# A macaron transformer layer on one core: queries' and keys' transfers behind a block's first loads, and a gap between the last scatter of a segment and its block

## The chip, the cores and the metric

One core of a Trainium2 chip runs the whole program. The metric is the device time of one execution in microseconds (us), as the median of several runs.

## The reference

Tokens are 32 batches of 256 rows with 128 features, so 8192 tokens or 64 tiles of 128. The layer has three parts, each with a residual:

```
x = x + 0.5 * moe(layernorm(x))        # 12 experts, 2 per token; 8 are real, 4 pass the token through
x = x + attention(layernorm(x))        # 16 heads of 8, scores + lambda * prior(|i - j|), softmax
x = x + 0.5 * moe(layernorm(x))        # the same weights again
```

A real expert is `silu(x @ w1.T) @ w2.T` with 256 hidden units. A token's two experts are the two largest gate logits, and their weights are a softmax over those two.

## The kernel before

**Segments and blocks.** The tokens of the first moe are cut into segments 0 to 4 (8, 8, 16, 16, 16 tiles) and those of the second into segments 5 to 9 (16, 16, 16, 8, 8). For each segment the kernel routes the tokens, scatters their normed rows into a table `xg` in DRAM that is sorted by expert (two indirect DMAs for each tile, `scatter_rows`, issued by GpSimd), and works through the table in groups of 256 rows (`experts`): 15 groups for a segment of 8 tiles, 23 for one of 16. Then it gathers each token's two result rows from a table `yg` (`gather_rows`, again two indirect DMAs for each tile) and adds them with their weights (`combine`, on VectorE). The passage through one segment's groups is called a block here, by the segment's number.

**A group in a block.** SyncE (SP) loads 256 rows transposed (`load_cols`, L313, into one of RX = 6 buffers `x_cols`). TensorE does `up` (L446 to L448), ScalarE does `silu` twice (L743, L745), VectorE subtracts to get the low part (L1168), TensorE does `down` two groups later (L461 to L464), ScalarE takes the result out of PSUM (`take_y`, L751, into one of RY = 4 buffers `y_rows`), and SP stores it (`store_y`, L322). SP issues in the written order: load g, then store g - 9. So store 0 comes behind load 9, and `take_y` of group 4 needs the buffer of store 0. Load g waits until `up` of group g - 6 is done.

**The next segment is routed inside a block.** VectorE takes the moments at its group 4, GpSimd computes the reciprocal root (`token_root`, L853 and L856), VectorE norms four tiles with each of its groups from 6 on (`token_norm`, L1052 and on), TensorE transposes them from its group 8 on (L396) and computes gate logits.

**Attention turns.** Attention runs in turns b = -1 to 32, one for each batch, each with 8 steps. A step has two score tiles of batch b (L548), two raw score tiles for the row maxima (L540), the prior added by matmuls (L573), exponentials (L807), maxima (L1276) and the product with the values (L602). The semaphore `st_done` counts 16 score tiles for each turn, and GpSimd's scatters and gathers are paced by it (`spread`). Each turn also projects the queries and keys of batch b + 2. SP then stores them (`keep_rows`) and reads them back in another layout with six DMAs (`operand_rows`, L353), into `k_op` and `q_in`. They are first read at step 3 of turn b + 1. `operand_rows(b + 2)` waits until all scores of turn b are done.

**Blocks among turns.** Turns and blocks share all engines, and each engine runs its program in the written order. `PHASES` says ahead of which turn a block stands and which segment it routes. Before a block, SP issues the block's first six loads at the end of its work for the turn, then `operand_rows`:

```
for b in range(-1, NBATCH - 2):
    if b in PHASES:
        experts(PHASES[b][0], RX)
    keep_rows(b + 2)
    if b + 1 in PHASES:
        for g in range(RX):
            load_cols(PHASES[b + 1][0], g)
    operand_rows(b + 2)
```

The first of these loads waits for all scatters of the segment (`scattered`). GpSimd's order is a list by hand. `spread(rows, q, t0, t1, b, steps, first)` issues the DMAs of tiles t0 to t1 evenly over `steps` steps from step `first` of turn b, with the norm of a coming batch (`batch_norm`, four instructions) once in each turn. `beside_block` issues them inside a block, and `norm_turns` only does the norms. `ADDS` says in which turns VectorE combines which tiles.

Of the kernel before, what the change touches and what calls it, by code (L numbers as in the profile page):

```python
# [43 lines left out]
def build(nc, x, wq, bq, wk, bk, wv, bv, wo, bo, lam, gate, ebias, w1, w2, ident, tri, prior, out, reach):  # L44
# [24 lines left out]
    RX, RY = 6, 4  # L69
# [5 lines left out]
    def through(counts):  # L75

        total = [0]
        for c in counts:
# [4 lines left out]
    T0 = through(n for _, n in SEG)  # L83
    K0 = through(n // 4 for _, n in SEG)

    PHASES = {4: (2, 3), 7: (3, 4), 11: (4, 5), 17: (5, 6), 25: (6, 7), 29: (7, 8)}

    ADDS = {-1: (0, 4, 8), 0: (1, 0, 2), 1: (1, 2, 6), 2: (1, 6, 8), 4: (2, 0, 4), 7: (2, 8, 12), 8: (2, 12, 16),
            29: (6, 0, 8), 30: (6, 8, 16)}
    for first, q in ((11, 3), (17, 4), (23, 5)):  # L90
        for i in range(4):
            ADDS[first + i] = (q, 4 * i, 4 * i + 4)

# [13 lines left out]
    with ExitStack() as ctx:  # L107
# [164 lines left out]
        def _(sp):  # L272
# [35 lines left out]
            def load_cols(q, g):  # L308
                n = G0[q] + g
                if g == 0:  # L310
                    sp.wait_ge(scattered[q % 2], landed(q))
                wait(sp, C["up_done"], n + 1 - RX)
                sp.dma_start_transpose(x_cols[:, n % RX], xg[q][g * GS:(g + 1) * GS, :]).then_inc(cols_in[n % RX], 16)  # L313
# [15 lines left out]
            out_tiles = out.rearrange("(n p) d -> p n d", p=P)  # L329
            AHEAD = RX + 3  # L330

            def experts(q, begun=0):
                for g in range(groups[q] + AHEAD):
                    if begun <= g < groups[q]:
                        load_cols(q, g)
                    if g >= AHEAD:
                        store_y(q, g - AHEAD)

# [8 lines left out]
            def operand_rows(b):  # L347

                sp.wait_ge(kq_out, 32 * (b + 1))
                wait(sp, A["st_done"], 16 * (b - 1))  # L350
                for dst, which, parts in ((k_op, 1, (0, 0, 1)), (q_in, 0, (0, 1, 0))):
                    for r in range(3):
                        sp.dma_start(  # L353
                            dst[r::4, b % 2, :, :],
                            kq_kept[:, 2 * parts[r] + which, :].rearrange("(g i) c -> i g c", g=G)).then_inc(kq_in[b % 2], 16)
# [8 lines left out]
            operand_rows(0)  # L364
            for b in range(-1, NBATCH - 2):
                if b in PHASES:
                    experts(PHASES[b][0], RX)
                keep_rows(b + 2)
                if b + 1 in PHASES:
                    for g in range(RX):  # L370
                        load_cols(PHASES[b + 1][0], g)
                operand_rows(b + 2)
                if b == 27:
                    store_out(5)
            store_out(6)
            experts(8)
# [458 lines left out]
        def _(pool):  # L835
# [130 lines left out]
            def norm_turns(b0, b1):  # L966
                for b in range(b0, b1):
                    batch_norm(b + 3)
# [6 lines left out]
            attention_constants()  # L975
            beside_block(gather_rows, 0, 0, 8, 1)
            norm_turns(-3, 0)
            spread(gather_rows, 1, 0, 8, 0, 16)
            spread(scatter_rows, 2, 0, 16, 2, 16)
            token_root(3)  # L980
            spread(gather_rows, 2, 0, 4, 4, 4)
            spread(scatter_rows, 3, 0, 16, 4, 20, 4)
            beside_block(gather_rows, 2, 4, 16, 3)
            spread(scatter_rows, 4, 0, 16, 7, 32)
            beside_block(gather_rows, 3, 0, 12, 4)
            spread(gather_rows, 3, 12, 16, 11, 8)
            spread(scatter_rows, 5, 0, 16, 12, 32)
            norm_turns(16, 17)
            beside_block(gather_rows, 4, 0, 12, 5)
            spread(gather_rows, 4, 12, 16, 17, 8)  # L990
            spread(scatter_rows, 6, 0, 16, 18, 32)
            spread(gather_rows, 5, 0, 12, 22, 24)
            beside_block(gather_rows, 5, 12, 16, 6)
            spread(scatter_rows, 7, 0, 16, 25, 32)
            beside_block(gather_rows, 6, 0, 16, 7)
            spread(scatter_rows, 8, 0, 8, 29, 8)
            spread(gather_rows, 7, 0, 12, 30, 16)
# [438 lines left out]
```

## Time and profile before

| | |
|---|---|
| median of 3 runs | 1392.34 us |
| lowest, highest | 1388.91, 1397.88 us |
| profiled execution | 1403.38 us, its span 1401.3 us |
| granted TensorE clock, mean | 0.88 |
| PE busy | 1003.8 us (72%) |
| DVE busy | 933.3 us (67%) |
| ACT busy | 665.9 us (48%) |
| POOL busy | 620.3 us (44%) |
| DMA | 125.29 MB, mean 89 GB/s |

PE is TensorE (PEld its weight loads), DVE VectorE, ACT ScalarE, POOL GpSimd, SP SyncE. Busy times leave out register, semaphore and DMA-issuing instructions; SPq and POOLq are the queues of those engines. Starts are counted from the beginning of the span, and L12 is line 12 of the kernel before.

### The profile page before, as it was taken

To read this page: it belongs to the slowest core of one execution; us is meant where nothing else is said; L and a number is where in the kernel's file an instruction comes from. 1 tells how busy PE (TensorE), PEld (TensorE's weight loads), DVE (VectorE), ACT (ScalarE), POOL (GpSimd) and SP (SyncE) were. 2 spreads that over 40 slices of the span, in tenths; PEclk is the share of its full clock that TensorE was granted. 3 is DMA by queue.
4 is the path that set the end of the run, shared out by engine and by line. 5 is a ranking of instruction groups with operands and counts; after the bars stand their busy time and mean duration, and the time that the engine had idled before them with its cause. 6 is when DMAs were issued, how large, how long until landed. Compare 5 with 4: busy or idle time off the path is not lost.

```text
span 1401.3 us, 37446 instructions
## 1 busy us (share of the span) xinstructions
PE 1003.8 (72%) x13558; PEld 658.8 (47%) x13558; DVE 933.3 (67%) x2505; ACT 665.9 (48%) x1356; POOL 620.3 (44%) x685
## 2 busy tenths in 40 slices
PE   1468177768776788688888888888888787775650
PEld 1346134447444744474445644444754464333540
DVE  5637476557665778578887778878688745646432
ACT  0146034346444655565555655555664554442540
POOL 2745135530555445444542555454224445541346
PEclk9979569889897989889999999999799978875985
DMA  8235812134113611262113721123431264140563
GB/s 246 70 103 126 256 41 60 54 80 107 54 52 90 139 47 58 75 143 69 47 58 72 148 73 47 58 58 81 106 84 49 84 140 101 50 86 18 117 155 74
DMA packets 248880, 125.29 MB, mean 89 GB/s; under 512 B 124384, under 2 KB 238925, under 8 KB 248448
## 3 DMA queue, kind: packets, MB, share of 16 engines
q1 hardware_dynamic: 232320, 94.01, 26.3%
q0 software_dynamic: 16384, 28.89, 8.6%
q8 instruction: 116, 1.90, 0.6%
q14 instruction: 60, 0.49, 0.1%
HBM read 36.25 MB, written 65.31 MB: 72 GB/s over the span
## 4 chain that ended last, share of the span: by engine, by line
PE 39%; DVE 25%; issue 14%; ACT 5%; POOL 5%; DMA 4%; another core or an unknown queue 4%; SPq 4%; POOLq 0%; DVEq 0%; ACTq 0%
DVE row_max L1276 9%; PE banks L573 8%; PE banks L602 4%; PE banks L548 3%; PE banks L446 3%; PE banks L448 2%; PE banks L405 2%; POOL big L888 2%; PE banks L540 2%; PE banks L447 2%; DVE h_lo L1168 2%; DMA x_cols<-xg 2%; PE banks L461 2%; PE banks L464 2%
## 5 line engine op out<-in xcount | busy, mean ns | idle before, releaser
L807 ACT ACTIVATE probs<-banks 128x512 f32<-128x512 f32 x512 | 279.5, 595 | 329.8 <-PE banks L573 301.8
L888 POOL DMA_INDIRECT big<-yg,slots x256 | 255.4, 998 | 384.2 <-ACT y_rows L751 184.9
L1276 DVE TENSOR_REDUCE row_max<-banks 128x2 f32<-128x512 f32 x512 | 330.4, 685 | 99.3 <-PE banks L573 73.2
L874 POOL DMA_INDIRECT xg<-xs,slots x256 | 259.5, 1014 | 277.5 <-PE banks L573 180.6
L1168 DVE TENSOR_TENSOR h_lo<-h_f,h_hi 128x512 bf16<-128x512 f32 x198 | 135.6, 688 | 182.1 <-ACT h_hi L745 154.5
L602 PE MATMUL banks<-probs,v_op 128*32 128x256 f32 x2048 | 196.9, 405 | 6.5 <-ACT probs L807 2.0
L461 PE MATMUL banks<-w_all,h_hi 128*128 x792 | 161.4, 231 | 52.5 <-DVE h_lo L1168 21.1
L540 PE MATMUL banks<-k_op,q_in 32*128 32x256 bf16 x1024 | 154.2, 290 | 57.8 <-DVE row_max L1276 39.9
L548 PE MATMUL banks<-q_op,k_op 32*128 32x256 bf16 x1024 | 151.3, 288 | 59.5 <-issue 45.2
L573 PE MATMUL banks<-band_parts,thirds 96*32 96x296 bf16 (+2 forms) x4096 | 184.0, 288 | 0.4 <-issue 0.4
L743 ACT ACTIVATE h_f<-banks 128x512 f32<-128x512 f32 x198 | 119.4, 603 | 130.4 <-PE banks L448 94.9
L446 PE MATMUL banks<-x_cols,w_all 128*128 128x256 bf16 x396 | 119.7, 302 | 78.0 <-DMA x_cols<-xg 47.1
L463 PE MATMUL banks<-w_all,h_hi 128*128 x792 | 157.0, 231 | 0.2
L464 PE MATMUL banks<-w_all,h_lo 128*128 x792 | 156.1, 230 | 1.3 <-issue 1.2
L573 PEld LDWEIGHTS banks<-band_parts,thirds 96*32 96x32 bf16 x4096 | 100.1, 98 | 62.1 <-issue 61.9
L751 ACT ACTIVATE y_rows<-banks 128x256 f32<-128x256 f32 x198 | 77.7, 393 | 102.6 <-PE banks L464 54.6
L448 PE MATMUL banks<-x_cols,w_all 128*128 128x256 bf16 x396 | 119.9, 303 | 0.9 <-issue 0.9
L447 PE MATMUL banks<-x_cols,w_all 128*128 128x256 bf16 x396 | 120.1, 303 | 0.4 <-issue 0.4
L745 ACT ACTIVATE h_hi<-banks 128x512 bf16<-128x512 f32 x198 | 119.4, 603 | 0.0
L461 PEld LDWEIGHTS banks<-w_all,h_hi 128*128 128x128 bf16 x792 | 82.3, 104 | 75.4 <-issue 71.3
L548 PEld LDWEIGHTS banks<-q_op,k_op 32*128 32x128 bf16 x1024 | 51.4, 92 | 130.9 <-issue 107.8
L602 PEld LDWEIGHTS banks<-probs,v_op 128*32 128x32 f32 x2048 | 81.7, 115 | 20.3 <-issue 13.3
(170 smaller groups left out, 1632.2 us busy)
## 6 DMA issues: line engine op xcount, KB each, us to landing
yg<-y_rows SPq DMA_DIRECT2D x198, 128.0 KB
k_op<-kq_kept SPq DMA_DIRECT2D x96, 64.0 KB
q_in<-kq_kept SPq DMA_DIRECT2D x96, 64.0 KB
xg<-zeros SPq DMA_DIRECT2D x2, 2944.0 KB, 14.4
xg<-xs,slots POOLq DMA_INDIRECT x256
big<-yg,slots POOLq DMA_INDIRECT x256
kq_kept<-kq_hi SPq DMA_DIRECT2D x32, 128.0 KB
kq_kept<-kq_lo SPq DMA_DIRECT2D x32, 128.0 KB
```

The source lines that it names most:

```text
L446: pe.matmul(o, w_hi, hi, start=True, stop=False)
L461: pe.matmul(o, h_hi[:, n % 4, cols], w_hi, start=c == 0 and j == 0, stop=False, skip_group_check=True)
L464: mm = pe.matmul(o, h_lo[:, n % 4, cols], w_hi, start=False, stop=c == 1, skip_group_check=True)
L540: return pe.matmul(banks[:, MX[v % 2], bass.ts(k, L)], q_in[r:r + 32, par, g, bass.ts(qt, P)], k_op[r:r + 32, par, g, :], start=k == 0, st ...
L548: return pe.matmul(banks[:, ST[(16 * b + u) % 3], bass.ts(k, L)], k_op[r:r + 32, par, g, bass.ts(kt, P)], q_op[r:r + 32, g, :], start=k == ...
L573: return pe.matmul(banks[32 * r:32 * r + 32, bank, :].rearrange("p (k c) -> p k c", k=2)[:, :, c0:c1], thirds[:], bc(band_parts[:, first:f ...
L602: mm = pe.matmul(banks[32 * j:32 * j + 32, PV, bass.ts(k, L)], v_op[:, par, kt, J * (2 * gp + k) + j, :], probs[:, w // 2 % 2, j, bass.ts( ...
L807: act.activation(probs[:, q % 2, u % 4, :], banks[:, ST[(16 * b + u) % 3], :], ACT.Exp).then_inc(A["exp_done"], 1)
L874: pool.indirect_dma_start(xg[q], bass.IndirectOffsetOnAxis(slots[:, q % 4, c, t:t + 1], 0), xs[:, q % 2, t, :], None, bounds_check=groups[ ...
L888: pool.indirect_dma_start(y_back[:, i, c, :], None, yg[q], bass.IndirectOffsetOnAxis(slots[:, q % 4, c, t:t + 1], 0)).then_inc(gathered[i] ...
L1168: dve.tensor_tensor(h_lo[:, n % 4, :], h_f[:, n % 3, :], h_hi[:, n % 4, :], ALU.subtract).then_inc(C["lo_ready"], 1)
L1276: dve.tensor_reduce(row_max[:, gp, :, qt, j], banks[:, MX[v % 2], :].rearrange("p (k c) -> p k c", k=2), AX.X, ALU.max).then_inc(A["max_do ...
```

## The change

The blocks that stood ahead of turns 11 and 17 stand ahead of turns 12 and 18. `ADDS` and the GpSimd list follow. In the GpSimd list the last scatter of a segment now comes before the end of the turn ahead of its block: for segments 2 and 3 in step 4 of that turn, for segment 4 a whole turn earlier (5 had this already), for segment 7 in step 3. For this, the scatters of segments 2 and 3 and the gathers of segment 1 are closer together in turns 0 to 6. Ahead of a block, SP no longer issues `operand_rows` behind the first six loads. It issues them inside the block, behind load 12 and ahead of store 3. The store of the finished segment 5 moves one turn back, behind the first loads of block 7.

```diff
-    PHASES = {4: (2, 3), 7: (3, 4), 11: (4, 5), 17: (5, 6), 25: (6, 7), 29: (7, 8)}
+    PHASES = {4: (2, 3), 7: (3, 4), 12: (4, 5), 18: (5, 6), 25: (6, 7), 29: (7, 8)}
...
-    for first, q in ((11, 3), (17, 4), (23, 5)):
+    for first, q in ((12, 3), (18, 4), (24, 5)):
...
-            def experts(q, begun=0):
+            def experts(q, begun=0, b=None):
                 for g in range(groups[q] + AHEAD):
                     if begun <= g < groups[q]:
                         load_cols(q, g)
+                    if b is not None and g == AHEAD + 3:
+                        operand_rows(b)
                     if g >= AHEAD:
                         store_y(q, g - AHEAD)
...
                 if b in PHASES:
-                    experts(PHASES[b][0], RX)
+                    experts(PHASES[b][0], RX, b + 1)
                 keep_rows(b + 2)
                 if b + 1 in PHASES:
                     for g in range(RX):
                         load_cols(PHASES[b + 1][0], g)
-                operand_rows(b + 2)
-                if b == 27:
+                else:
+                    operand_rows(b + 2)
+                if b == 28:
                     store_out(5)
...
-            spread(gather_rows, 1, 0, 8, 0, 16)
-            spread(scatter_rows, 2, 0, 16, 2, 16)
+            spread(gather_rows, 1, 0, 8, 0, 11)
+            spread(scatter_rows, 2, 0, 16, 1, 18, 3)
+            norm_turns(3, 4)
             token_root(3)
             spread(gather_rows, 2, 0, 4, 4, 4)
-            spread(scatter_rows, 3, 0, 16, 4, 20, 4)
+            spread(scatter_rows, 3, 0, 16, 4, 17, 4)
+            norm_turns(6, 7)
             beside_block(gather_rows, 2, 4, 16, 3)
             spread(scatter_rows, 4, 0, 16, 7, 32)
+            norm_turns(11, 12)
             beside_block(gather_rows, 3, 0, 12, 4)
-            spread(gather_rows, 3, 12, 16, 11, 8)
-            spread(scatter_rows, 5, 0, 16, 12, 32)
-            norm_turns(16, 17)
+            spread(gather_rows, 3, 12, 16, 12, 8)
+            spread(scatter_rows, 5, 0, 16, 13, 32)
+            norm_turns(17, 18)
             beside_block(gather_rows, 4, 0, 12, 5)
-            spread(gather_rows, 4, 12, 16, 17, 8)
-            spread(scatter_rows, 6, 0, 16, 18, 32)
-            spread(gather_rows, 5, 0, 12, 22, 24)
-            beside_block(gather_rows, 5, 12, 16, 6)
-            spread(scatter_rows, 7, 0, 16, 25, 32)
+            spread(gather_rows, 4, 12, 16, 18, 8)
+            spread(scatter_rows, 6, 0, 16, 19, 32)
+            spread(gather_rows, 5, 0, 8, 23, 16)
+            beside_block(gather_rows, 5, 8, 16, 6)
+            spread(scatter_rows, 7, 0, 16, 25, 28)
+            norm_turns(28, 29)
```

## Rows read from the trace of the kernel before

**Rows 1.** Timeline of PE, first matmul of blocks 2 to 7 (start, us, idle before)

```profile
293.59 0.39 PE L446 MATMUL banks<-x_cols,w_all 128*128 128x256 bf16 x1 [8.26 <-DMA x_cols<-xg]
...
433.90 0.39 PE L446 MATMUL banks<-x_cols,w_all 128*128 128x256 bf16 x1 [7.37 <-DMA x_cols<-xg]
...
579.40 0.39 PE L446 MATMUL banks<-x_cols,w_all 128*128 128x256 bf16 x1 [5.41 <-DMA x_cols<-xg]
...
761.33 0.28 PE L446 MATMUL banks<-x_cols,w_all 128*128 128x256 bf16 x1 [1.82 <-issue]
...
979.11 0.39 PE L446 MATMUL banks<-x_cols,w_all 128*128 128x256 bf16 x1 [2.37 <-issue]
...
1120.04 0.39 PE L446 MATMUL banks<-x_cols,w_all 128*128 128x256 bf16 x1 [5.29 <-DMA x_cols<-xg]
```

**Rows 2.** Timeline of SP at block 2

```profile
290.93 7.78 SPq L313 DMA_TRANSPOSE x_cols<-xg  x6
298.82 2.65 SPq L353 DMA_DIRECT2D k_op<-kq_kept  x3
...
303.45 5.19 SPq L313 DMA_TRANSPOSE x_cols<-xg  x4
308.69 0.58 SPq L322 DMA_DIRECT2D yg<-y_rows  x1
```

**Rows 3.** Timeline of SP at block 6

```profile
981.52 5.20 SPq L313 DMA_TRANSPOSE x_cols<-xg  x4
986.81 1.07 SPq L322 DMA_DIRECT2D yg<-y_rows  x1
```

**Rows 4.** Timeline of PE, group 6 of blocks 2, 4 and 7

```profile
306.28 0.39 PE L446 MATMUL banks<-x_cols,w_all 128*128 128x256 bf16 x1 [3.07 <-DMA x_cols<-xg]
...
592.82 0.39 PE L446 MATMUL banks<-x_cols,w_all 128*128 128x256 bf16 x1 [3.88 <-DMA x_cols<-xg]
...
1132.77 0.39 PE L446 MATMUL banks<-x_cols,w_all 128*128 128x256 bf16 x1 [2.71 <-issue]
```

**Rows 5.** Timeline of ACT: group 4 in blocks 2 and 6, 7 in 6

```profile
310.83 0.38 ACT L751 ACTIVATE y_rows<-banks 128x256 f32<-128x256 f32 x1 [1.97 <-DMA yg<-y_rows]
...
989.51 0.38 ACT L751 ACTIVATE y_rows<-banks 128x256 f32<-128x256 f32 x1
...
997.82 0.38 ACT L751 ACTIVATE y_rows<-banks 128x256 f32<-128x256 f32 x1 [1.00 <-PE banks L464]
```

**Rows 6.** Line L751, blocks 2, 5, 6, 7: ns of one, first to last start

```profile
L751 ACT ACTIVATE y_rows<-banks x23: 384/385/416, 299.2 to 351.0; 128x256 f32<-128x256 f32 x23
...
L751 ACT ACTIVATE y_rows<-banks x23: 384/390/431, 765.4 to 813.2; 128x256 f32<-128x256 f32 x23
...
L751 ACT ACTIVATE y_rows<-banks x23: 384/384/415, 983.8 to 1034.2; 128x256 f32<-128x256 f32 x23
...
L751 ACT ACTIVATE y_rows<-banks x23: 377/385/465, 1125.5 to 1180.8; 128x256 f32<-128x256 f32 x23
```

**Rows 7.** Timeline of POOL, the root in blocks 2 and 6

```profile
304.92 2.94 POOL L856 TENSOR_TENSOR rstd<-var_eps,neg_half 128x16 f32<-128x16 f32 x1
...
989.71 3.26 POOL L856 TENSOR_TENSOR rstd<-var_eps,neg_half 128x16 f32<-128x16 f32 x1
```

**Rows 8.** Line L548 in turns 3, 5 and 9, first to last score matmul

```profile
L548 PE MATMUL banks<-q_op,k_op x32: 264/278/417, 257.1 to 283.6; 32*128 32x256 bf16 x32
...
L548 PE MATMUL banks<-q_op,k_op x32: 265/278/416, 378.2 to 399.8; 32*128 32x256 bf16 x32
...
L548 PE MATMUL banks<-q_op,k_op x32: 264/278/278, 535.6 to 552.4; 32*128 32x256 bf16 x32
```

**Rows 9.** Window of block 5: us, five engines' busy us, PEclk, DMA share, GB/s

```profile
761.30:813.20 51.90, 40.99 (x479) 34.21 (x479) 40.60 (x131) 32.77 (x73) 26.95 (x24) 1.00 0.65 137
```

**Rows 10.** Timeline of POOL at block 2, the last four scatters

```profile
284.78 1.06 POOL L874 DMA_INDIRECT xg<-xs,slots  x1 [0.17 <-issue]
...
288.72 0.98 POOL L874 DMA_INDIRECT xg<-xs,slots  x1 [0.30 <-issue]
```

## The prediction

> **What bounds the kernel now.** I read the page first. No engine is busy for much more than 7 tenths of the span, so the time is made of waits at the seams between stages, and the question is which seam the change touches. It touches the entries of six blocks and the first half of each block, so I next read the timeline of PE at each entry [rows 1]. The bracket is the idle time ahead of the block's first matmul. In blocks 2, 3, 4 and 7 it is 8.26, 7.37, 5.41 and 5.29 us and ended by the landing of the first load. In blocks 5 and 6, whose scatters were through one or several turns earlier, it is 1.82 and 2.37 us and ended by nothing that waits for data. The chain names why: at block 2 the last scatter starts at 288.72 [rows 10], the first load is issued at 290.93 [rows 2], so 2.2 us later, and the first matmul starts at 293.59, another 2.7 us later. The last scatters stand behind the last turn's work in time: SP's first load waits for them, and PE has long finished the turn.
>
> The second place is group 6 of a block. PE waits there 3.07, 3.88 and 2.71 us in blocks 2, 4 and 7 [rows 4]; block 3 repeats it. SP's timeline shows the cause: six loads take 7.78 us to issue, then `operand_rows` takes from 298.82 to 303.45, 4.63 us, and only then comes load 6 [rows 2]. The delay goes on: store 0 stands behind load 9 and is issued at 308.69, and ScalarE takes group 4's result at 310.83, after 1.97 us of idle that the store's landing ended [rows 5]. In block 6 the same chain runs 7 us earlier relative to its first matmul: load 6 at 981.52, store 0 at 986.81 [rows 3], and group 4's result has no wait [rows 5]. So blocks 5 and 6 are measured samples of a block that finds its first loads landed.
>
> How much a block would shorten is read from ScalarE's takes of results [rows 6] against the first matmul [rows 1]: from first matmul to last take block 2 needs 351.0 - 293.6 = 57.4 us (blocks 3 and 4 are two more like it), block 7 1180.8 - 1120.0 = 60.8, block 5 813.2 - 761.3 = 51.9, and block 6 1034.2 - 979.1 = 55.1.
>
> **The change part by part.** The sum is made against the profiled execution, 1403.4 us (span 1401.3 plus 2.1 around it). It is 11 us above the median; nothing in the terms depends on where these 11 us lie, so the difference is carried over to the median.
>
> *Entries.* With the last scatter paced at step 4 of the turn ahead (step 3 for block 7, a whole turn for block 4), three steps remain. A turn of 21.6 us [rows 8] has steps of 2.7 us, so some 8 us remain, against 2.2 us from the last scatter to the first load and 2.7 us to the first matmul. The loads go out 1.3 us apart (7.78 / 6), which is at least as fast as PE needs them. What is late next is what ends the entries of blocks 5 and 6: 2.1 us as a mean. Gain: 8.26 + 7.37 + 5.41 + 5.29 - 4 x 2.1 = 17.9 us. Bounds: 12 us, if one of the deepest two keeps its wait, to 17.9.
>
> *The body of blocks 2, 3, 4 and 7.* Load 6 now needs only `up` of group 0 and is issued about a microsecond into the block, and store 0 right behind load 9. That is block 6's pattern or better. Not all of the wait at group 6 comes back, because another chain runs beside it: moments, root, norm, transposes. The root starts 304.92 - 293.59 = 11.3 us after the first matmul in block 2 and 989.71 - 979.11 = 10.6 in block 6 [rows 7], so it hardly noticed the wait. I therefore take the whole body, not the waits: 53.5 us, the mean of blocks 5 and 6. Three blocks x (57.4 - 53.5) + the same 3.9 for block 7 = 15.6 us. Bounds: 0 (the chain of the root sets the body) to 4 x 5.5 = 22 (all as block 5), and 3.2 more if block 6 falls to block 5 too.
>
> *`operand_rows` inside the block.* The six DMAs are not removed: 4.63 us of SP's time come between load 12 and store 3, in all six blocks. Queued behind them on SP are stores 3 and on and loads 13 and on. Load 13 has time, since its group comes many groups later. Store 3 has not: ScalarE needs its buffer for group 7. From a first matmul at 0, `up` of group 3 ends near 5, load 9 is issued until 6.4, and each pair of a load (5.19 / 4 = 1.30) and a store (0.58) takes 1.9 [rows 2], so load 12 ends at about 12.2, `operand_rows` at 16.8, and store 3 has landed 310.83 - 308.69 = 2.1 us later, at 18.9. In block 6 group 7's result was taken at 997.82 - 979.11 = 18.7, ended by PE and not by a store [rows 5]. So the cover is used up within 0.2 us. I put 1 us on each of six blocks, 6 us lost; bounds 0 and 4.63 each. The reader of the transferred rows is step 3 of the next turn, more than 30 us later, and doesn't notice.
>
> *Denser turns.* From first to last score matmul turn 9, with 8 scatters, takes 16.8 us, turn 5 with 12.8 takes 21.6, and turn 3 with 16 takes 26.5 [rows 8]. Above 8 a scatter costs (21.6 - 16.8) / 4.8 = 1.0 us by the first pair. The new list has 11.6, 13.3, 14.2 and 8.9 DMAs in turns 0 to 3 where there were 8, 8, 16, 16, and 15.5, 15.1, 9.4 in turns 4 to 6 where there were 14.4, 12.8, 12.8. The excess over 8 is 3.6 + 5.3 + 6.2 + 0.9 + 7.5 + 7.1 + 1.4 = 32.0 us against 0 + 0 + 8 + 8 + 6.4 + 4.8 + 4.8 = 32.0. I take 0. Turn 3 alone is 9.7 above turn 9 and not 8, so packing may be worth 2 us, or cost 13 (below).
>
> *The rest.* Blocks at turns 12 and 18, their `ADDS`, and the gathers of segment 5 (8 beside turns instead of 12, 16 beside block 6 instead of 8) do the same work at other turns; block 5 had 24 gathers beside it and was the shortest. Taken at 0. The 1 MB store of segment 5 now goes out behind block 7's first loads, which cover it; without the cover it costs another wait like those of [rows 4], 3 us.
>
> Sum: -17.9 - 15.6 + 6 + 0 = -27.5. The profiled execution comes to 1403.4 - 27.5 = 1375.9 us, the median to 1392.3 - 27.5 = 1364.8, so 1365 us.
>
> **The rivals.**
>
> *A. The root's chain takes the body's gain.* The root starts at the same 11 us in blocks 2 and 6 [rows 7], and norm, transposes and gate logits follow it group by group. If it sets the body, that gain is nil: -17.9 + 6 = -11.9, or with the 4 us that block 6 shows at least for half the blocks, -16: 1376 us. For it: the root's row. Against it: block 5 had that chain too and needed 5.5 us less than block 2. Chance 0.16.
>
> *B. Denser turns cost more than the line says.* If turns 1, 2, 4 and 5 (13.3 to 15.5 DMAs) each cost turn 3's 9.7 us, the excess is 3.6 + 4 x 9.7 + 0.9 + 1.4 = 44.7 instead of 32.0, 12.7 us lost: 1377.5 us. Chance 0.09.
>
> *C. The change doesn't make the gap.* GpSimd falls behind its paces, and in blocks 2, 3 and 7 the last scatter still ends after the turn. Four scatters start 3.94 us apart in all, 1.3 us each [rows 10], so 14.2 of them are 18.6 us of a turn of some 24, and with the turn's norm it is nearly full. Then only block 4 gains its 3.3 at the entry, and the body's 15.6 and the 6 stay: -12.9, 1379 us. Chance 0.07.
>
> *D. Slower: the stores are held in all six blocks.* If store 3 lands 4.63 us late for ScalarE in each block, and store 4 and on follow it at 1.9 us a pair, the loss is 6 x 4.63 = 27.8 us, and the body's gain goes with it, since the wait only moved from group 6 to group 7: -17.9 + 27.8 = +9.9, 1402 us. It decides where store 3 lands later than ScalarE comes to group 7, which is within 0.2 us of even by the estimate above; but the loss grows only with the excess over that point, and ScalarE's group 7 waits for PE anyway. DMA traffic could push it over: in block 5 the engines' share was 0.65 [rows 9]. The Trainium skill, DMA: Bandwidth & Descriptors, Issuing engines are not separate DMA queues, says that DMAs of all issuing engines run on the same 16 DMA engines and interleave. By that rule the six transfers slow the loads, stores and gathers in the block's middle, where in the kernel before they met only the loads, and the sum would be this rival's; block 5's trace shows a full DMA load without a long body, which speaks against it. Chance 0.03.
>
> **How the numbers follow.** Forecast 0.63, A 0.16, B 0.09, C 0.07, D 0.03, and 0.02 for more than all gains. The likeliest is 1365. Low end: entries 17.9, bodies 22 + 3.2, insertion 0, turns -2, in sum -45: 1347, taken as 1349. High end: A, B and C end at 1376 to 1379, with a little insertion more 1382. One per cent is 14 us, about what a measurement of this kernel can tell from no change. Forecast, most of A and half of B lie beyond it (below 1378.4): faster 0.86. Same: most of C, the rest of A and B, and a milder D, 0.11. Slower 0.03.
>
> **What the new profile would show.** The first matmul of blocks 2, 3, 4 and 7 has under 3 us of idle ahead of it, with no DMA as its end. SP's first loads lie before the turn's last matmul. Group 6 doesn't wait for `x_cols`. `operand_rows` stands behind load 12 and ends near 17 us, and ScalarE's take of group 7 shows whether it waits for a store. Last take minus first matmul is 52 to 55 us. Turns 0, 1 and 5 are longer, 3 and 6 shorter, in sum even. The prediction is wrong if the entries keep a DMA wait, if the bodies stay at 57 us, or if turns 0 to 6 grow by more than 5 us together.

## The result and the profile after

The changed kernel takes 1374.55 us, median of 5 runs (1371.88 to 1381.74), beside 1390.67 us for the kernel before (5 runs, 1387.69 to 1397.88). The ratio is 0.989 (0.986 to 0.992): 16.1 us or 1.1% faster. The forecast was 1365, 27.5 us less. The profiled execution took 1381.74 us against 1403.38, so the two traces compared below differ by 21.6 us, and the medians by less.

The page after, its span and its busy times:

```profile
span 1379.5 us, 37446 instructions
...
PE 1006.4 (73%) x13558; PEld 653.6 (47%) x13558; DVE 932.2 (68%) x2505; ACT 664.9 (48%) x1356; POOL 622.2 (45%) x685
```

The work is the same to within 3 us on each engine. What changed is waiting, so it must be looked for by place. First the timeline of PE, the first matmul of blocks 2 to 7, which answers to [rows 1]:

```profile
289.60 0.28 PE L449 MATMUL banks<-x_cols,w_all 128*128 128x256 bf16 x1 [1.82 <-issue]
...
430.79 0.28 PE L449 MATMUL banks<-x_cols,w_all 128*128 128x256 bf16 x1 [1.82 <-issue]
...
585.38 0.33 PE L449 MATMUL banks<-x_cols,w_all 128*128 128x256 bf16 x1 [1.82 <-issue]
...
761.63 0.28 PE L449 MATMUL banks<-x_cols,w_all 128*128 128x256 bf16 x1 [1.82 <-issue]
...
962.21 0.39 PE L449 MATMUL banks<-x_cols,w_all 128*128 128x256 bf16 x1 [2.31 <-issue]
...
1104.74 0.39 PE L449 MATMUL banks<-x_cols,w_all 128*128 128x256 bf16 x1 [1.83 <-issue]
```

No entry waits for a DMA any more. Blocks 2, 3, 4 and 7 had 26.33 us of idle ahead of them and have 7.29. Block 5 seems to stand as it stood, 761.63 where it was 761.33, but it now has one turn more ahead of it (turn 17, 18.9 us). The first score matmul of turn 18, which lies behind block 5 in both kernels, shows the gain so far. On the timeline of PE it is, before and after:

```profile
835.20 0.36 PE L548 MATMUL banks<-q_op,k_op 32*128 32x256 bf16 x1 [0.98 <-issue]
...
814.02 0.27 PE L551 MATMUL banks<-q_op,k_op 32*128 32x256 bf16 x1 [0.52 <-issue]
```

That is 21.2 us earlier, nearly all of the 21.8 us by which the span is shorter. Blocks 2 to 5 together are 26.2 us shorter, from the last matmul of the turn ahead to the first of the next. So the turns up to there have given some of it back, and why they did is the question of the experiments.

SP at block 2 after, to be read beside [rows 2]:

```profile
284.79 13.87 SPq L313 DMA_TRANSPOSE x_cols<-xg  x10
298.71 0.59 SPq L322 DMA_DIRECT2D yg<-y_rows  x1
...
304.85 1.89 SPq L355 DMA_DIRECT2D k_op<-kq_kept  x3
306.79 1.90 SPq L355 DMA_DIRECT2D q_in<-kq_kept  x3
308.73 0.59 SPq L322 DMA_DIRECT2D yg<-y_rows  x1
```

The first load is issued 4.8 us ahead of the first matmul, where it was 2.7. `operand_rows` takes 3.8 us behind load 12 and ends 19.1 us into the block. Store 3 is issued at 308.73, so late that ScalarE waits for it at group 7. Block 3 has such a wait too, of 0.70 us; the timeline of ACT shows it for blocks 2, 4 and 6:

```profile
310.95 0.38 ACT L754 ACTIVATE y_rows<-banks 128x256 f32<-128x256 f32 x1 [3.31 <-DMA yg<-y_rows]
...
607.45 0.38 ACT L754 ACTIVATE y_rows<-banks 128x256 f32<-128x256 f32 x1 [1.54 <-DMA yg<-y_rows]
...
985.05 0.38 ACT L754 ACTIVATE y_rows<-banks 128x256 f32<-128x256 f32 x1 [2.95 <-DMA yg<-y_rows]
```

Blocks 5 and 7 have no such wait. The takes of results, blocks 2, 5, 6 and 7 as in [rows 6]:

```profile
L754 ACT ACTIVATE y_rows<-banks x23: 384/384/391, 293.6 to 346.1; 128x256 f32<-128x256 f32 x23
...
L754 ACT ACTIVATE y_rows<-banks x23: 384/390/440, 765.7 to 813.5; 128x256 f32<-128x256 f32 x23
...
L754 ACT ACTIVATE y_rows<-banks x23: 384/387/466, 967.8 to 1015.0; 128x256 f32<-128x256 f32 x23
...
L754 ACT ACTIVATE y_rows<-banks x23: 384/390/465, 1109.5 to 1165.2; 128x256 f32<-128x256 f32 x23
```

From first matmul to last take the six blocks need 56.5, 51.7, 53.0, 51.9, 52.8 and 60.4 us, in sum 326.3, where it was 339.5. The gain is not spread as forecast: blocks 2 and 7 are 0.9 and 0.3 us shorter, blocks 3 and 4 together 9.7, block 6 2.3. Entries and bodies together are 32.3 us shorter. The span is only 21.8 shorter. The difference lies in the turns. I add up, for each turn, the time from its first score matmul to its last value product: turns 0 to 6 have 177.2 us (166.2 before), turns 24 to 28 106.7 (96.9), all others 403.6 (412.0), so 12.3 more in sum. The score matmuls of turns 3, 5 and 9, beside [rows 8]:

```profile
L551 PE MATMUL banks<-q_op,k_op x32: 264/278/416, 263.8 to 285.7; 32*128 32x256 bf16 x32
...
L551 PE MATMUL banks<-q_op,k_op x32: 264/278/417, 375.0 to 400.6; 32*128 32x256 bf16 x32
...
L551 PE MATMUL banks<-q_op,k_op x32: 264/278/278, 525.7 to 542.7; 32*128 32x256 bf16 x32
```

Turn 3 fell from 26.5 to 21.9 with 8.9 DMAs in place of 16, but turn 5 rose from 21.6 to 25.6. Turn 6 shows how such a turn loses its time. The timeline of PE in its middle:

```profile
405.17 0.64 PE L576 MATMUL banks<-band_parts,thirds 96*32 96x296 bf16 x16
...
409.63 0.77 PE L576 MATMUL banks<-band_parts,thirds 96*32 96x296 bf16 x10
411.50 0.46 PE L576 MATMUL banks<-band_parts,thirds 96*32 96x244 bf16 x3 [1.10 <-issue]
412.23 0.43 PE L576 MATMUL banks<-band_parts,thirds 96*32 96x296 bf16 x1 [0.28 <-issue]
412.97 0.37 PE L576 MATMUL banks<-band_parts,thirds 96*32 96x244 bf16 x2 [0.31 <-issue]
414.44 1.09 PE L605 MATMUL banks<-probs,v_op 128*32 128x256 f32 x8 [1.10 <-issue]
```

The sixteen matmuls of one prior are one row of 0.64 us at 405.17. From 409.63 on the same sixteen come in four pieces over 3.7 us, and no semaphore ends the pauses. The timeline of POOL over the same stretch:

```profile
406.75 0.97 POOL L877 DMA_INDIRECT xg<-xs,slots  x1 [0.30 <-issue]
...
409.30 0.97 POOL L877 DMA_INDIRECT xg<-xs,slots  x1 [0.30 <-issue]
...
412.13 0.97 POOL L877 DMA_INDIRECT xg<-xs,slots  x1 [0.30 <-issue]
```

GpSimd issues seven scatters from 404.11 to 412.13, almost without a pause; with the run's end the matmuls come in whole rows again. This is the theory that the experiments test: **(M) a run of scatters issued back to back holds the other engines up, and it is the run that costs, not the number of scatters in a turn.** GpSimd comes into such runs when it is behind its paces, for instance after a norm. Its rivals: the cost goes by the number in a turn; GpSimd's own norm is late and PE waits for it; the turns' length is chance of one execution; two DMAs paced at one step collide.

### The profile page after: what moved, and what is told of

Read it like the earlier page. It is cut to its first block, busy times and chain, and to the rows that moved or that the text cites. A ratio compares the mean times of both kernels' runs of the same rounds, so it can differ in the third digit from the quotient of the medians.

```text
span 1379.5 us, 37446 instructions
## 1 busy us (share of the span) xinstructions
PE 1006.4 (73%) x13558; PEld 653.6 (47%) x13558; DVE 932.2 (68%) x2505; ACT 664.9 (48%) x1356; POOL 622.2 (45%) x685
## 4 chain that ended last, share of the span: by engine, by line
PE 40%; DVE 25%; issue 13%; ACT 6%; another core or an unknown queue 6%; SPq 4%; POOL 3%; DMA 2%; DVEq 0%; POOLq 0%; ACTq 0%
DVE row_max L1283 10%; PE banks L576 9%; PE banks L605 4%; PE banks L551 3%; PE banks L451 3%; PE banks L449 2%; PE banks L543 2%; POOL big L891 2%; PE banks L467 2%; PE banks L408 2%; DVE h_lo L1175 2%; PE banks L464 2%; PE banks L450 2%; PE banks L466 2%
## 5 line engine op out<-in xcount | busy, mean ns | idle before, releaser
L605 PE MATMUL banks<-probs,v_op 128*32 128x256 f32 x2048 | 202.6, 414 | 10.6 <-issue 4.5
L464 PE MATMUL banks<-w_all,h_hi 128*128 x792 | 159.1, 229 | 55.6 <-DVE h_lo L1175 26.7
L576 PE MATMUL banks<-band_parts,thirds 96*32 96x296 bf16 (+2 forms) x4096 | 189.2, 293 | 2.1 <-issue 2.1
L746 ACT ACTIVATE h_f<-banks 128x512 f32<-128x512 f32 x198 | 119.7, 605 | 106.6 <-PE banks L451 65.6
L466 PE MATMUL banks<-w_all,h_hi 128*128 x792 | 154.3, 229 | 0.5 <-issue 0.4
L449 PE MATMUL banks<-x_cols,w_all 128*128 128x256 bf16 x396 | 118.0, 298 | 50.1 <-issue 14.6
L450 PE MATMUL banks<-x_cols,w_all 128*128 128x256 bf16 x396 | 118.4, 299 | 1.1 <-issue 1.1
L451 PE MATMUL banks<-x_cols,w_all 128*128 128x256 bf16 x396 | 118.2, 298 | 0.4 <-issue 0.4
```

The costliest lines, as they stand in the source:

```text
L464: pe.matmul(o, h_hi[:, n % 4, cols], w_hi, start=c == 0 and j == 0, stop=False, skip_group_check=True)
L466: pe.matmul(o, h_hi[:, n % 4, cols], w_lo, start=False, stop=False, skip_group_check=True)
L576: return pe.matmul(banks[32 * r:32 * r + 32, bank, :].rearrange("p (k c) -> p k c", k=2)[:, :, c0:c1], thirds[:], bc(band_parts[:, first:f ...
L605: mm = pe.matmul(banks[32 * j:32 * j + 32, PV, bass.ts(k, L)], v_op[:, par, kt, J * (2 * gp + k) + j, :], probs[:, w // 2 % 2, j, bass.ts( ...
```

## The experiments

Each kernel is an edit of the changed kernel, and each ratio is to the kernel before on the same chip. Four chips were used: one for the first four kernels (kernel before: 1383.97), one for the next four (1387.59), one for three (1391.4), one for the last (1293.25). "Turns 0 to 6" and the like mean the sum defined above; "the blocks" is the sum over blocks 2 to 7 from the last matmul of the turn ahead to the first of the next turn (372.9 before, 340.6 after).

**1. The SP part alone.** GpSimd's list, `PHASES` and `ADDS` are those of the kernel before; `operand_rows` goes into the block.

```diff
-    PHASES = {4: (2, 3), 7: (3, 4), 12: (4, 5), 18: (5, 6), 25: (6, 7), 29: (7, 8)}
+    PHASES = {4: (2, 3), 7: (3, 4), 11: (4, 5), 17: (5, 6), 25: (6, 7), 29: (7, 8)}
...
-            spread(scatter_rows, 2, 0, 16, 1, 18, 3)
-            norm_turns(3, 4)
+            spread(scatter_rows, 2, 0, 16, 2, 16)
```

> The kernel before with one part alone: operand_rows of a block's turn is issued behind load 12 and not behind the first six loads. The waits at the entries should stay (26.3 us in blocks 2, 3, 4 and 7 together). Theory S (the late loads 6 to 9 set the body): from first matmul to last take blocks 2, 3, 4 and 7 fall by 3 to 5 us each, and the time by 10 to 16 us, ratio 0.990. Rival R (the root and norm chain sets the body): the wait at group 6 goes, but the bodies stay within 1 us and the ratio is 1.000.

Measured: 1380.72 us, ratio 0.998 (0.995 to 1.001). Block 2's entry is as before, on the timeline of PE:

```profile
292.37 0.39 PE L449 MATMUL banks<-x_cols,w_all 128*128 128x256 bf16 x1 [8.35 <-DMA x_cols<-xg]
```

The waits for loads at group 6 are gone in all blocks, but ScalarE now waits for store 3 at group 7, by 4.44, 4.59, 2.41 and 2.38 us in blocks 2, 3, 4 and 6. The bodies sum to 329.2 us, but no gain can be told in the time. The edit to SP alone is worth nothing that can be measured; the interval leaves room for 7 us.

**2. The gap alone.** `operand_rows` stands again behind the first six loads; everything else is the changed kernel.

```diff
-                    experts(PHASES[b][0], RX, b + 1)
+                    experts(PHASES[b][0], RX)
...
-                else:
-                    operand_rows(b + 2)
+                operand_rows(b + 2)
```

> The changed kernel without its SP part: the GpSimd list, ADDS and the blocks at 12 and 18 stay, operand_rows stands again behind the first six loads. Block 5 took 54.2 us before the change with this order and 54.2 after it, so if the gap alone gives what the bodies gained, the ratio is that of the changed kernel, 0.989 to 0.992, with idle of 1.8 us ahead of each block. Rival: the bodies need the SP part even with early loads; then blocks 2, 3, 4 and 7 are 3 us longer each and the ratio is 0.998.

Measured: 1362.26 us, 0.986 (0.982 to 0.990), the whole gain. SP at block 2, whose first matmul is at 287.18:

```profile
279.40 8.49 SPq L313 DMA_TRANSPOSE x_cols<-xg  x6
287.99 1.89 SPq L353 DMA_DIRECT2D k_op<-kq_kept  x3
289.92 1.90 SPq L353 DMA_DIRECT2D q_in<-kq_kept  x3
```

The gap lets SP start 7.8 us ahead of PE, and so the six DMAs are over 4.6 us into the block, where they ended 9.9 us into it before [rows 1, 2]. That is not early enough everywhere: the wait at group 6 is 0.40 us in block 2, but 2.21 in block 3 and 3.80 in block 7, on the timeline of PE:

```profile
1101.43 0.28 PE L446 MATMUL banks<-x_cols,w_all 128*128 128x256 bf16 x1 [3.80 <-DMA x_cols<-xg]
```

The bodies sum to 317.2 us. With the SP part they sum to 326.3 in the first trace and 319.8 in kernel 4's, the same kernel, so two executions differ by more than the SP part can be seen to change.

**3. The early gap undone.** Turns 0 to 6 have the list of before.

```diff
-            spread(gather_rows, 1, 0, 8, 0, 11)
-            spread(scatter_rows, 2, 0, 16, 1, 18, 3)
-            norm_turns(3, 4)
+            spread(gather_rows, 1, 0, 8, 0, 16)
+            spread(scatter_rows, 2, 0, 16, 2, 16)
...
-            spread(scatter_rows, 3, 0, 16, 4, 17, 4)
-            norm_turns(6, 7)
+            spread(scatter_rows, 3, 0, 16, 4, 20, 4)
```

> The changed kernel with the list of turns 0 to 6 as before (no gap and no closer scatters for segments 2 and 3). Theory D (closer indirect DMAs cost 11 us in turns 0 to 6): turns 0 to 6 return to 166 us together from 177, blocks 2 and 3 lose their entries' 12 us, and the ratio is as the changed kernel's, 0.989. Rival N (the longer turns were chance of one execution): turns 0 to 6 are equal in both, and this kernel is 10 to 12 us slower than the changed one, ratio 0.997.

Measured: 1376.58 us, 0.996 (0.994 to 0.999). Blocks 2 and 3 need 124 us against 107 in the next kernel, turns 0 to 6 170.1 against 175.6. The early gap is worth 17 us at the blocks and costs 5 in the turns; the whole is 13.7 us slower without it.

**4. The changed kernel again**, unedited, on this chip.

> The changed kernel once more, for a second profile. Theory D: turns 0 to 6 again sum to 175 to 180 us. Turns 24 to 27, which were 88 us against 78 before although their work is nearly the same, fall back to 80 or less if that was chance of the clock, and stay at 88 if the new place of segment 5's combines and the scatters of segment 7 cause it.

Measured: 1362.93 us, 0.986 (0.982 to 0.990), within 1 us of the gap alone. Turns 0 to 6 need 175.6 us, turns 24 to 28 100.0. So the longer turns 0 to 6 repeat: the three traces with the old list there have 166.2, 167.8 and 170.1, the eight with the new one (after and kernels 2 and 4 to 9) 172.7 to 177.7. On this chip that is 5 to 8 us, not 10.9.

**5. Segment 7 as before.**

```diff
-            spread(scatter_rows, 7, 0, 16, 25, 28)
-            norm_turns(28, 29)
+            spread(scatter_rows, 7, 0, 16, 25, 32)
```

> The changed kernel with segment 7's scatters over 32 steps as before (no gap ahead of block 7). Theory D (a turn pays about 1 us for each indirect DMA above 8): turns 24 to 28, 100 to 107 us in four kernels with the new list and 96 to 97 in two with the old one, fall back to 97 or 98, the entry of block 7 is 5.3 us again instead of 1.8, and the ratio stays within 0.003 of the changed kernel's. Rival (the combines of segment 5, moved to turns 24 to 27, are the cost): turns 24 to 28 stay at 100 or more and the kernel is 4 to 6 us slower than the changed one.

Measured: 1366.76 us, 0.987 (0.984 to 0.990). Turns 24 to 28 need 96.7 us against 100.0 in kernel 4, block 7 65.6 against 61.8. This gap gives and takes alike. The combines of segment 5 still stand in turns 24 to 27 here, so it isn't they that made these turns longer.

**6. Eight scatters in one run.** The changed kernel has 8 scatters of segment 5 in each of turns 13 to 16, one for each step, and these are among its shortest turns. The same 8 are now issued back to back, from step 2 on, and the norm behind them.

```diff
-            spread(scatter_rows, 5, 0, 16, 13, 32)
+            for i in range(4):
+                at = 16 * (13 + i) + 4
+                for t in range(4 * i, 4 * i + 4):
+                    scatter_rows(5, t, t + 1, (A["st_done"], at, at))
+                batch_norm(16 + i)
```

> The changed kernel, with segment 5's scatters (8 in each of turns 13 to 16) no longer spread one to a step but all eight back to back from step 1 of each turn. Theory M (a run of back-to-back indirect DMAs on GpSimd in steps 1 to 4 holds PE up): turns 13 to 16, now 77 us together, take 90 us or more, with idle of ScalarE and VectorE that no engine's instruction ends. Rival C (what costs is the count in a turn, above 8): 77 to 79 us, as now.

Measured: 1399.21 us, 1.010 (1.007 to 1.013). Turns 13 to 16 need 111.0 us, 34 more than the 77.0 of kernel 4, or 8.4 a turn, with the same 8 scatters in each. The timeline of PE in turn 14, while POOL issues eight scatters 1.28 us apart from 683.33 to 692.39:

```profile
687.54 0.63 PE L605 MATMUL banks<-probs,v_op 128*32 128x256 f32 x5 [0.44 <-issue]
...
695.84 0.37 PE L551 MATMUL banks<-q_op,k_op 32*128 32x256 bf16 x1 [3.41 <-issue]
```

Windows of this turn (us, busy us of PE, PEld, DVE, ACT and POOL, PEclk, DMA share, GB/s), ahead of the run and in it:

```profile
681.00:683.00 2.00, 1.73 (x35) 0.92 (x35) 1.26 (x3) 0.98 (x3) 0.00 (x0) 1.00 0.35 97
687.00:689.00 2.00, 0.78 (x10) 0.27 (x6) 0.00 (x0) 0.00 (x1) 1.43 (x2) 1.00 0.14 47
691.00:693.00 2.00, 0.60 (x4) 0.38 (x4) 0.00 (x0) 0.00 (x0) 1.58 (x2) 0.96 0.14 48
```

In the run PE does less than half of its work, and DVE and ACT next to none. The DMA engines are busy for 0.14 of the time, so it isn't their bandwidth. The granted clock is full, so it isn't the clock. No row in the run waits for the norm. The number in a turn isn't the cause of these 34 us: it is the same. Whether it costs something too is another question, and the kernel before bears on it. Its turn 3 took 28.2 us with its scatters mostly in pairs, as on the timeline of POOL:

```profile
269.28 0.98 POOL L874 DMA_INDIRECT xg<-xs,slots  x1 [1.70 <-PE banks L573]
270.57 0.98 POOL L874 DMA_INDIRECT xg<-xs,slots  x1 [0.31 <-issue]
272.11 0.98 POOL L874 DMA_INDIRECT xg<-xs,slots  x1 [0.56 <-PE banks L573]
273.40 0.98 POOL L874 DMA_INDIRECT xg<-xs,slots  x1 [0.30 <-issue]
```

That is 9 us more than a turn of 13 to 16 with single scatters, and without a long run, though other work of this early turn may have a share in it. Kernel 8 has such pairs in turns 13 and 14.

**7. The run later in the turn**, from step 6 on, with the norm behind the fourth scatter.

```diff
+                at = 16 * (13 + i) + 12
+                for t in range(4 * i, 4 * i + 2):
+                    scatter_rows(5, t, t + 1, (A["st_done"], at, at))
+                batch_norm(16 + i)
+                for t in range(4 * i + 2, 4 * i + 4):
+                    scatter_rows(5, t, t + 1, (A["st_done"], at, at))
```

> As the burst at step 1, but from step 5 of each of turns 13 to 16, with the turn's norm after four of the eight. If steps 5 to 7 have no work that such a run disturbs (they kept their length in dense turns), turns 13 to 16 stay at 77 to 79 us; if any run of scatters holds PE up, they take 90 us like the burst at step 1.

Measured: 1379.54 us, 0.996 (0.993 to 1.000). Turns 13 to 16 need 87.4, 10 more than with one scatter a step. POOL issues two runs of up to four for each turn, 1.29 us apart, and they cost three tenths of one run of eight. The edit changes the place of the runs and their length at once, so it doesn't tell which of the two makes them cheaper.

**8. Sixteen in a turn.** Segment 5's scatters go out in turns 13 and 14 alone, paced evenly.

```diff
-            spread(scatter_rows, 5, 0, 16, 13, 32)
-            norm_turns(17, 18)
+            spread(scatter_rows, 5, 0, 16, 13, 16)
+            norm_turns(15, 18)
```

> The changed kernel with segment 5's 32 scatters over 16 steps (turns 13 and 14, 16 in each) and none in turns 15 and 16: density alone, away from blocks and from the ramp. Theory D: turns 13 and 14 take 25 to 28 us each and 15 and 16 stay at 19, in sum 12 to 16 us more than now, ratio 0.01 above the changed kernel's. Rival: packing costs nothing by itself and the early turns are long for another reason; then the four turns stay at 77 to 80 us.

Measured: 1384.01 us, 0.999 (0.996 to 1.002). Turns 13 to 16 need 26.0, 28.3, 22.9 and 18.0, 18 more in sum. The prediction's line gives 16, for 2 x 8 scatters above 8. GpSimd issues them in pairs and in one run of four behind the norm, so this kernel doesn't tell the count from the runs by itself. It shows that packing costs, and that the turns left without scatters of their own give next to nothing back: turn 16 is 1.1 us shorter than in kernel 4, turn 15 3.4 us longer.

**9. The second of two DMAs later.** Where `spread` paces both DMAs of a tile at one step, the second waits for the values' product of that step, and not for its second score tile.

```diff
+                    if same:
+                        paces = ((A["st_done"], 16 * b + 2 * at[0] + 1), (A["pv_done"], 8 * b + at[0] - 1))
+                        rows(q, t, t + 1, paces)
```

> The changed kernel, where the second of two indirect DMAs that are due in the same step waits for the step's product with the values instead of the step's second score tile, so that pairs in denser turns are further apart. Theory M (PE stands while GpSimd issues indirect DMAs back to back): turns 0 to 6 fall from 176 us towards 170 and turns 24 to 28 from 103 towards 99, ratio 0.003 to 0.007 below the changed kernel's. Rival (catching up after the norm makes the runs, not the pairs): turns 0 to 6 stay at 174 to 177.

Measured: 1368.12 us, 0.983 (0.978 to 0.987); turns 0 to 6 177.7, as long as ever, and the ratio's interval overlaps that of kernel 4. But the edit didn't do what it was for. The timeline of POOL in turn 5:

```profile
373.00 0.99 POOL L879 DMA_INDIRECT xg<-xs,slots  x1 [0.67 <-PE banks L576]
374.29 0.98 POOL L879 DMA_INDIRECT xg<-xs,slots  x1 [0.31 <-issue]
375.57 0.98 POOL L879 DMA_INDIRECT xg<-xs,slots  x1 [0.30 <-issue]
```

The DMAs still go out 1.28 us apart, so this kernel says nothing on what the pairs cost.

**10. At most one tile in flight, beside turns.** The first DMA of a tile also waits for the landing of the tile before.

```diff
+                        if t and c == 0 and paced and paced[0] is A["st_done"]:
+                            pool.wait_ge(scattered[q % 2], landed(q) - 32 * SEG[q][1] + 32 * t)
                         pool.indirect_dma_start(
```

> The changed kernel, where in the attention turns GpSimd issues the first indirect DMA of a tile only when both of the tile before have landed: no run is longer than two, at the same count in a turn as far as the pace allows (a pair then takes some 3.5 us, so 14 a turn is about the limit). Theory M: turns 1 to 3, 5 and 6 fall by 1 to 3 us each, sum of turns 0 to 6 168 to 172, but the last scatters of segments 2 and 3 may come late and give back some us at these two entries. Rival C (the count in a turn costs, not the run): turns 0 to 6 stay at 174 to 177.

Measured: 1425.2 us, 1.025 (1.021 to 1.029). A pair now goes out every 4.3 to 4.7 us at the quickest, and turns 4 and 5 fall to 20.6 and 21.4 us, from 25.3 and 26.4 in kernel 4. But 9 and 8 DMAs are issued in them and not 13 and 14, so runs and number fell together. Turns 1 to 3, with 14, 10 and 12 DMAs nearly all in such pairs, take 26.9, 24.0 and 25.2 us, no less than the 25.4, 24.5 and 26.3 of kernel 4, where M had forecast 1 to 3 us less each. So the first half of M, that a run costs, stands on kernel 6; the second, that the number doesn't, is not shown. GpSimd also gets too slow for its list, and turn 6 takes 37.0, as the timeline of PE says:

```profile
421.64 0.69 PE L526 MATMUL banks<-ident_f,a_xn 128*128 128x128 f32 x2 [13.74 <-POOL a_xn L941]
```

The norm of the coming batch stands behind the scatters on GpSimd. The entries of blocks 2 and 3 wait for their last scatter again, 13.1 and 13.2 us.

**11. The same beside blocks too**: the condition on `st_done` is left out.

```diff
+                        if t and c == 0:
```

> The same limit beside blocks too. Theory M: block 7, with 32 gathers beside it, falls from 59 to 63 us towards 56, blocks 4 and 5 by up to 1 us; the first segments' scatters at the start, which no turn hides, become some 5 to 10 us slower, so that the whole is no faster than with the limit in turns alone. Rival: blocks keep their length and only the start loses.

Measured: 1514.34 us, 1.087 (1.083 to 1.091). Block 7 falls to 53.2 us, where the other kernels with the new list have 58 to 63. It has 32 gathers beside it, and on the chip of kernel 12, where runs cost nothing, its body is 52.1 us. So the gathers' runs are a likely reason why it stays the longest block. The blocks ahead of the turns and those behind them wait for their gathers and scatters: PE stands 58.5 us in one wait at the end. Limiting the rate costs far more than it gives where GpSimd's rate bounds.

**12. A smaller gap**, after what 3 and 5 showed: less packing.

```diff
-            spread(scatter_rows, 2, 0, 16, 1, 18, 3)
-            norm_turns(3, 4)
+            spread(scatter_rows, 2, 0, 16, 1, 20, 3)
...
-            spread(scatter_rows, 3, 0, 16, 4, 17, 4)
-            norm_turns(6, 7)
+            spread(scatter_rows, 3, 0, 16, 4, 19, 4)
...
-            spread(scatter_rows, 7, 0, 16, 25, 28)
-            norm_turns(28, 29)
+            spread(scatter_rows, 7, 0, 16, 25, 30)
```

> The changed kernel with gaps two steps smaller: the last scatters of segments 2, 3 and 7 are due in step 6, 6 and 5 of the turn ahead of their block instead of 4, 4 and 3. They need 2.2 us to the first load and 2.7 to the first matmul, about two steps. Theory D: the scatters are less close (12.8, 13.5 and 8.5 a turn instead of 14.2, 15.1 and 9.1), turns 0 to 6 fall from 176 to about 172 and turns 24 to 28 from 103 to 100, and if the entries keep under 2.5 us each, the ratio is 0.003 to 0.005 below the changed kernel's. Rival: the entries of blocks 2 and 3 wait again for data, 2 to 5 us each, and the ratio is that of the changed kernel or above it.

Measured: 1270.13 us, 0.982 (0.979 to 0.986), on a chip where the kernel before takes 1293.25 and not 1384 to 1391. There the premise is gone. The timeline of POOL in turn 1, a run like the others, and the last scatters of segment 3:

```profile
207.67 0.98 POOL L877 DMA_INDIRECT xg<-xs,slots  x1 [0.30 <-issue]
...
368.08 0.97 POOL L877 DMA_INDIRECT xg<-xs,slots  x1 [0.30 <-issue]
369.36 0.97 POOL L877 DMA_INDIRECT xg<-xs,slots  x1 [0.30 <-issue]
```

The timeline of PE beside it, with matmuls in whole rows:

```profile
207.70 0.64 PE L576 MATMUL banks<-band_parts,thirds 96*32 96x296 bf16 x16
208.12 0.66 PE L605 MATMUL banks<-probs,v_op 128*32 128x256 f32 x8
...
374.38 0.39 PE L449 MATMUL banks<-x_cols,w_all 128*128 128x256 bf16 x1 [5.94 <-DMA x_cols<-xg]
```

Turns 1, 2, 5 and 6 take 19.7, 19.1, 17.8 and 17.7 us. In turn 5 GpSimd issues 14 scatters 1.28 us apart from start to end, and the turn is as short as the shortest: here neither the run nor the number costs the other engines anything that shows.

The last row of PE is the entry of block 3: it waits 5.94 us again (block 2 3.16). The last scatter of segment 3 starts at 369.36, though it is paced at step 6 of turn 6, and that turn's last value product starts at 367.80. From turn 5 on GpSimd pauses only for its norms. At 1.28 us each it can't issue what the list asks of a turn of 17.7 us, so it is GpSimd's rate that closes the gap there, which is the mechanism of rival C. What the full gap does on this chip wasn't measured, and whether less packing pays on the other chips is not told by this run either.

## Why the prediction came out as it did

**Entries: right.** -17.9 forecast, -19.0 in the two traces. What is late next is what ended the entries of blocks 5 and 6, as the step said. This holds on chips where a turn is long enough for GpSimd to issue in it all that the list asks (kernel 12).

**Bodies and insertion: near in size, wrong in cause and in place.** -15.6 + 6 = -9.6 forecast, -13.2 in the two traces; but two executions of the changed kernel differ by 6.5 us in this sum (326.3 and 319.8), so the nearness is in part luck. The step gave 3.9 us to each of blocks 2, 3, 4 and 7 and forecast 52 to 55 us from first matmul to last take. Block 2 kept 56.5 us; SP started only 4.8 us ahead of it, and in kernel 4, where it started 7.7 us ahead, the body is 51.0. Block 7 kept 60.4 (59.5 in kernel 4), probably for the reason that kernel 11 points at. `operand_rows` ends 19 us into block 2 where the step had 17, and the waits for store 3 sum to 8.5 us where the step had 6. The text gave the bodies' gain to the move of `operand_rows`. Kernel 2 has it without the move, and kernel 1, with the move alone, has no measurable gain. With the gap, SP starts earlier and the wait at group 6 shrinks or goes; the insertion then trades what is left of it for a wait at group 7 (3.31 us in block 2). Kernels 2 and 4 are level.

**Denser turns: the step that failed.** It was taken as 0 because the line of excess over 8 gave 32.0 on both sides; turns 3 and 6 were to win back what turns 1 and 5 lose. They didn't. Turn 3 went from 28.2 to 24.0 us, 4.2 less, for 7.1 fewer DMAs, and turn 6, which had 3.4 fewer, from 24.2 to 26.1. Turn 1 rose from 19.7 to 26.2, turn 5 from 23.7 to 27.3. Turns 0 to 6 grew by 10.9 us in the two traces, and by 5 to 8 where both lists stood on one chip (kernels 1 to 4). The prediction named growth by more than 5 us as a sign of being wrong, and this sign came. A slope through three turns says nothing of why a DMA costs. Kernel 6 shows that 8 scatters cost 8.4 us more or nothing, by how they are issued, which no count can tell. The term's own bound, up to 13 lost, held it, and rival B had the sign and nearly the size, by a price for each dense turn. How the growth divides between runs and number is open: kernel 9 left the pairs as they were, and kernel 10 changed both.

**The rest, taken at 0: too low by a few us.** Segment 7's scatters went from 8 to 9.1 a turn, and the step didn't count them. Turns 24 to 28 went from 96.9 to 106.7; undoing it gives 96.7 (kernel 5), and the other traces with the new list have 100.0 to 104.0 (kernels 2 to 4 and 6 to 9). The prediction's own line would have given 3.4.

**The other rivals.** A: the bodies did shorten, though the root's chain was not tested by itself. C: all entries lost their DMA wait, so the gap was there, except on the chip of kernel 12. D: store 3 was late in blocks 2, 3, 4 and 6, by 3.3, 0.7, 1.5 and 3.0 us, and the bodies still gained. The working carried over the 11 us by which the profiled execution of before stands above its median of 3. By the five runs it is 12.7, and after it is 7.2, which is the difference between 21.6 and 16.1 and lies in no term. Between the forecast of 27.5 and the 21.6 of the two traces stand +12.3 for the turns, -4.7 for entries, bodies and insertion together, and -1.7 for all that lies between turns, ahead of turn 0 and behind turn 31.

## What to carry to other kernels

Where a stage starts by loading what the stage ahead has scattered, put the last scatter two or three steps ahead of the seam and look whether the idle ahead of the first matmul still ends by a DMA; the gap gives its gain twice, at the entry and by letting the loading queue finish its other DMAs earlier. Pay for it with steps that have one indirect DMA each, and not by packing: when GpSimd falls behind its paces it issues in runs, and in kernel 6 eight in a run stretched a turn by 8.4 us where the same eight one by one did not. Sixteen in a turn, most of them in pairs, stretched it as much (kernel 8). Before a gap is sized, compare what GpSimd is asked to issue in a turn with its 1.28 us for each DMA, for the shortest turn on any chip, and test each part of a combined edit alone: here one part carried all. After such a trial, look whether the edit changed what it was meant to, and compare places in two traces only where the same work lies ahead of them.

## What the hardware showed that was not expected

In the traces of every chip but the last the other engines crawl while GpSimd issues indirect DMAs 1.28 us apart without a pause. Seven in a row show it in turn 6 above, eight cost 8.4 us a turn (kernel 6), four and four 2.6 (kernel 7). PE, DVE and ACT stop without a semaphore of the program as the cause, at a DMA share of 0.14 and a granted clock of 0.96 to 1.00. On the last chip even 14 in a row cost nothing that shows (turn 5 of kernel 12, 17.8 us), and the kernel before takes 1293 us instead of 1384 to 1391. The waits of kernel 12's trace name no unknown source at all, while at ScalarE's exponentials alone kernel 4 has 34.5 us that end so, and kernel 6 56.5. That much is shown.

What the engines wait for is not shown. The Trainium skill, SBUF — State Buffer, section SBUF: two separate sides, says that on the engines' side of SBUF only the port pair that VectorE and GpSimd share can be fought over, and that TensorE and ScalarE never wait on anyone there. By that rule the pair could hold VectorE up, but not PE and ACT; the windows of kernel 6 have PE at 0.60 us of 2.00 and ACT at none, so it is not this alone. Bandwidth, the clock and the norm are excluded by the same rows. No run here separates what is left, and the cause stays open. So does how much of the change's gain goes with the chip: the changed kernel gained 1.1 and 1.4% in its two measurements, the near variant 12 1.8% on the last chip.
